# The last two head pairs of slot attention inside the opening order of cross-attention

## The chip, the cores and the metric

The kernel runs on one core of a Trainium2 chip. The metric is the device time of one execution in microseconds (us). TensorE (PE) multiplies; PEld is its weight load, which runs beside it. VectorE (DVE), ScalarE (ACT) and GpSimd (POOL) work on what it leaves in the eight PSUM banks, and SyncE (SP) issues DMAs. Every engine runs its own instruction stream in order, and the streams meet only at semaphores.

## The reference, cut to what matters

One decoder layer on x of 8 sequences x 128 tokens x 256 channels:

```
x = x + slot_attention(layernorm(x))     # 16 heads of 128, 64 slots
x = x + cross_attention(layernorm(x), ctx)   # 32 heads of 8
x = x + experts(layernorm(x))            # 8 experts (2 chosen) + 1 shared
```

Slot attention, for each head (q and k have rotary positions):

```
s  = clip(hs @ Ws1.T @ Ws2.T + bs2);  es = exp(s);  enz = 1 / cumsum(es)
ok = enz * (mask(q k^T) @ es)
W2 = mask((softmax(ok) * enz) @ es^T)
o  = rmsnorm(W2 @ v) * silu(g);  y += o @ Wo.T
```

## The kernel before

The 16 heads are worked on as 8 pairs, the 8 sequences of a pair in 4 groups of two. A pair has projection steps and attention steps. Projections fill a PSUM bank each: QK 0 to 7 (q and k, each then rotated by VectorE and GpSimd), VG 0 to 7 (v and gate of a sequence), ST and SN (slot scores, both ways), CS 0 and 1 (running sums of es). ScalarE takes a logarithm of CS, then an exponential, to get `enz`; before it, it loads the table set that has the logarithm, and after CS 1 the set that has the tanh of VG. The attention steps of group g are, on TensorE: A (q k^T), E (times es), T (transpose), W (W2), O (times v), OT (transpose), Y (times Wo, in three products of high and low parts). Between them other engines mask, scale, exponentiate, square and norm. All A write bank 2, E and Y share bank 3, T and OT share bank 4, W uses bank 5, and O banks 6 and 7 in turn. Tiles between the engines have two buffers, chosen by the group's number modulo 2.

Every engine has a list of steps written out in its order. In turn i of the loop (`Fori(1, PAIRS - 2)`) the attention of pair i runs beside the projections of pair i + 1. After the loop one more turn of the same order is written out for pair 6 (with the projections of pair 7). Then come lists of the next stage: `X_PE_START`, `X_DVE_START`, `X_ACT_START`, `X_POOL_START` and `X_SP_START`, here called the opening. They hold the attention of pair 7 (steps "7A" to "7Y", "7N2" the second norm's statistics) mixed with the first steps of cross-attention for sequences 0, 1 and 2. These are G 0 to 6 (projections and the stacks of q and k, turned), H (norm), L1 (logits, whose maxima VectorE takes: line 1458), TT (the maxima turned), a DMA that puts them into the rows of q (`QT`, line 1278), L2 (logits again, less the maxima; ScalarE exponentiates them), AV, AB, AT and OUT (the output), S3, HN and HT (third norm), and GT, the first expert product (from line 1395 on). WH and WL split the experts' weights of expert b into high (ScalarE) and low parts (GpSimd, lines 1680 and 1681). After GT of sequence 0 the regular turns `X_PE` begin, one for each sequence.

The steps of the opening that need a free PSUM bank are `FILLERS`; `bank_plan()` hands out the bank that has been free longest, so banks 0 and 1 first and the others when the attention has left them (`FREED`). Raw weights of the next stage lie in places of tiles that the projections leave. The steps FREE and LATE of SyncE wait until the last projection is through (`projections_done`) and then issue nine DMAs in a row, 4.1 MB. Line 248 to 250 are the three products of high and low parts wherever they occur.

## Time and profile before

| | |
|---|---|
| runs of the kernel (3) | 610.56, 611.94, 614.62 us; median 611.94 |
| profiled execution, its own time | 614.3 us |
| its span, first to last instruction | 612.5 us |
| busy share of the span | PE 95%, DVE 79%, ACT 60%, POOL 46% |
| mean granted TensorE clock | 0.983 |

All times within an execution count from the start of its span. A clock of 1.00 is 2.4 GHz, and 0.5 is 1.2 GHz. The busy time of TensorE includes the drain of a matmul, which overlaps the next one, so a busy share of 0.9 is less work than 0.9 of the stretch, and at half clock the same work shows as twice the busy time.

### The profile page before, as it was taken

How to read it: one execution, taken by the hardware profiler on the slowest of the kernel's cores; microseconds unless marked ns; L12 is line 12 of the kernel's file. 1: busy time of each engine (PE TensorE's matmuls, PEld its weight loads, DVE VectorE, ACT ScalarE, POOL GpSimd, SP SyncE). 2: the span in 40 equal slices, each digit the busy share in tenths (PEclk: the TensorE clock that was granted, in tenths of full speed). 3: DMA queues.
4: the chain of work that ended last, by engine and by line, in shares of the span. 5: the costliest groups of instructions: out<-in, count | busy, mean ns of one | idle time of the engine just before them, and what ended most of it. 6: DMA issues, size and time to landing. Idle time of an engine off the chain costs nothing.

```text
span 612.5 us, 14139 instructions
## 1 busy us (share of the span) xinstructions
PE 581.9 (95%) x4426; PEld 490.9 (80%) x4426; DVE 486.6 (79%) x1150; ACT 369.8 (60%) x1166; POOL 281.9 (46%) x324
## 2 busy tenths in 40 slices
PE   5989999999999999999999999986889999999998
PEld 5868888888888888888888888774668878877786
DVE  5999978887977977977986986775687887886776
ACT  3448566647657557557567555756666576567453
POOL 3366844754845755663663664545562211220000
PEclk9999999999999999999999999987799999999999
DMA  8200101101100100200200000700000000000000
GB/s 273 70 0 34 55 1 39 50 1 34 51 0 32 54 0 0 86 0 0 86 0 1 18 2 1 276 2 1 3 3 11 2 12 11 3 11 12 3 10 18
DMA packets 10321, 19.35 MB, mean 32 GB/s; under 512 B 2336, under 2 KB 5920, under 8 KB 10144
## 3 DMA queue, kind: packets, MB, share of 16 engines
q1 hardware_dynamic: 10272, 18.74, 8.9%
q8 instruction: 26, 0.43, 0.3%
q14 instruction: 23, 0.19, 0.1%
HBM read 17.55 MB, written 1.05 MB: 30 GB/s over the span
## 4 chain that ended last, share of the span: by engine, by line
PE 81%; DVE 8%; issue 5%; DMA 2%; POOL 1%; ACT 1%; SPq 1%; DVEq 0%; POOLq 0%; ACTq 0%
PE bank L248 16%; PE bank L250 15%; PE bank L249 15%; PE bank L589 4%; PE bank L546 3%; PE bank L1359 3%; PE bank L581 3%; PE bank L558 3%; PE bank L599 2%; PE bank L1288 2%; PE bank L1348 2%; PE bank L1336 2%; PE bank L1407 1%; PE bank L1306 1%; PE bank L1366 1%
## 5 line engine op out<-in xcount | busy, mean ns | idle before, releaser
L845 ACT ACTIVATE sa_v<-bank 128x256 f32<-128x256 f32 x64 | 24.4, 382 | 66.9 <-PE bank L250 66.8
L908 POOL TENSOR_TENSOR sa_qt<-sa_rope_cos,sa_rope_sin 128x512 f32<-128x512 f32 x32 | 41.2, 1286 | 42.2 <-DVE sa_rope_sin L760 42.0
L819 ACT ACTIVATE sa_ex<-sa_okb,sa_minus_top 128x64 f32<-128x64 f32 x128 | 42.9, 339 | 24.9 <-DVE sa_minus_top L712 24.9
L248 PE MATMUL bank<-ht_hi,sa_qk_hi 128*128 128x512 f32 x128 | 55.4, 432 | 1.0 <-DVE sa_gate L765 0.9
L908 POOL TENSOR_TENSOR sa_kt<-sa_rope_cos,sa_rope_sin 128x512 f32<-128x512 f32 x32 | 41.2, 1289 | 30.7 <-DVE sa_rope_sin L760 30.7
L248 PE MATMUL bank<-sa_vg_hi,ht_hi 128*128 128x512 f32 x128 | 52.6, 411 | 0.5 <-DVE sa_rope_sin L760 0.5
L250 PE MATMUL bank<-sa_vg_hi,ht_lo 128*128 128x512 f32 x128 | 50.5, 395 | 0.0
L250 PE MATMUL bank<-ht_hi,sa_qk_lo 128*128 128x512 f32 x128 | 50.5, 394 | 0.0
L249 PE MATMUL bank<-sa_vg_lo,ht_hi 128*128 128x512 f32 x128 | 50.5, 394 | 0.0
L249 PE MATMUL bank<-ht_lo,sa_qk_hi 128*128 128x512 f32 x128 | 50.2, 392 | 0.0
L758 DVE TENSOR_TENSOR sa_rope_cos<-bank,con 128x512 f32<-128x512 f32 x64 | 44.0, 687 | 6.0 <-PE bank L250 5.5
L1458 DVE TENSOR_REDUCE xf_neg_top<-bank 128x4 f32<-128x512 f32 x64 | 40.3, 682 | 9.3 <-PE bank L1336 9.1
L759 DVE TENSOR_TENSOR sa_rope_sin<-bank,con 64x512 f32<-64x512 f32 x64 | 44.3, 692 | 0.9
L760 DVE TENSOR_TENSOR sa_rope_sin<-bank,con 64x512 f32<-64x512 f32 x64 | 43.8, 684 | 0.8
L1657 POOL TENSOR_TENSOR xf_rot<-xf_by_cos,xf_by_sin 128x256 f32<-128x256 f32 x16 | 12.1, 756 | 65.2 <-DVE xf_by_sin L1451 65.2
L914 POOL TENSOR_TENSOR sa_qe<-sa_ex,sa_enz 128x256 f32<-128x256 f32 x32 | 23.4, 731 | 39.2 <-ACT sa_ex L819 39.2
L1557 ACT ACTIVATE xf_wt<-bank 128x512 f32<-128x512 f32 x64 | 34.1, 600 | 8.1 <-PE bank L1348 8.1
L248 PE MATMUL bank<-sa_wo_hi,sa_ogt_hi 128*128 128x256 f32 x128 | 38.4, 300 | 0.0
L831 ACT ACTIVATE sa_junk<-bank 128x128 f32<-128x128 f32 x128 | 33.7, 282 | 6.5 <-PE bank L589 6.5
L765 DVE SCALAR_TENSOR_TENSOR sa_gate<-sa_th,bank 128x256 f32<-128x256 f32 x64 | 26.5, 417 | 13.6 <-ACT sa_th L848 5.7
L546 PEld LDWEIGHTS bank<-sa_qt,sa_kt 128*128 128x128 f32 x256 | 32.3, 191 | 5.8 <-DVE sa_att L703 3.7
L726 DVE SCALAR_TENSOR_TENSOR sa_og<-bank,sa_rms,sa_gate 128x128 f32<-128x128 f32 x128 | 35.8, 343 | 1.3 <-POOL sa_rms L927 1.1
(207 smaller groups left out, 1840.7 us busy)
## 6 DMA issues: line engine op xcount, KB each, us to landing
sa_qk_raw<-in_wqk SPq DMA_DIRECT2D x8, 512.0 KB, 3.8
sa_vg_raw<-in_wvg SPq DMA_DIRECT2D x8, 512.0 KB, 3.2
sa_wo_raw<-in_wo SPq DMA_DIRECT2D x8, 256.0 KB, 2.7
xf_w_raw<-in_w SPq DMA_DIRECT2D x2, 640.0 KB, 11.1
xf_w_raw<-in_w SPq DMA_DIRECT2D x1, 1152.0 KB, 9.6
xs<-in_x SPq DMA_DIRECT2D x2, 512.0 KB, 4.6
hn<-in_w SPq DMA_DIRECT2D x2, 512.0 KB, 4.9
out<-xs SPq DMA_DIRECT2D x8, 128.0 KB, 1.7
```

What stands on the lines that cost most here:

```text
L248: pe.matmul(out, w_hi, m_hi, start=first, stop=False)
L249: pe.matmul(out, w_hi, m_lo, start=False, stop=False)
L250: return pe.matmul(out, w_lo, m_hi, start=False, stop=last)
L546: mm = pe.matmul(ps_a[:, u * TOK:(u + 1) * TOK], kt[:, h, b * TOK:(b + 1) * TOK], qt[:, h, b * TOK:(b + 1) * TOK], start=True, stop=True)
L726: ins = dve.scalar_tensor_tensor(out=og[:, s, u, :], in0=ps_o[s][:, u * DK:(u + 1) * DK], scalar=rms[:, s, u:u + 1], in1=gate[:, b, h * DK ...
L758: dve.tensor_tensor(rope_cos[:, s, :].rearrange("p (b t) -> p b t", b=4), psv, cos4, ALU.mult)
L759: dve.tensor_tensor(rs[0:64], psv[64:128], sin4[64:128], ALU.mult)
L760: dve.tensor_tensor(rs[64:128], psv[0:64], sin4[0:64], ALU.mult).then_inc(draining, 1)
L819: ins = act.activation(ex[:, s, u, :], okb[:, s, u, :], ACT.Exp, bias=minus_top[:, s, u:u + 1], accum_out=total[:, g, u:u + 1])
L908: pool.tensor_tensor(dst[:, h, c * HALF:(c + 1) * HALF], rope_cos[:, s, :], rope_sin[:, s, :], ALU.add).then_inc(roped, 1)
L1458: dve.tensor_reduce(neg_top[:, b % 2, n % 4, 4 * (n // 4):4 * (n // 4) + 4], bank(filled(step, n, b), 0, 512, 4), AX.X, ALU.max, negate=Tr ...
L1557: act.activation(wt[:, n, :, :], bank(filled(step, n, b), 0, 512, 4), ACT.Exp, scale=XDIM ** -0.5).then_inc(exp_done, 1)
```

## The change

The turn of pair 6 is no longer a turn of the loop's order. Its steps, attention of pair 6 and projections of pair 7, stand in the opening's lists as "6A", "6QK" and so on, and all lists of the opening are new orders. Attention goes by groups across both pairs in the order `LAST_ORDER`: 6.0, 6.1, 6.2, 7.0, 7.1, 6.3, 7.2, 7.3. The counters of the semaphores and the choice of the buffer of two follow that order (`group`, `at`, `buffer_of`). As E and Y, and T and OT, of the two pairs now mix, each waits for whatever stood before it in its shared bank (`shared_banks`). Pair 7 has its own buffer of `wo_hi` and `wo_lo` (`wo_set`). The projections of pair 7 become fillers with banks from `bank_plan()`. CS 0 and CS 1 stand apart on ScalarE with VG steps between them, so that each gets its own load of the logarithm's table set and is followed by one of the tanh's set.

The tiles `qk_hi`, `qk_lo`, `rope_cos` and `rope_sin` moved into the region that is freed late. So the DMAs of the next stage fall into two lots: FREE (wq, the first four experts' w1 and w3, gate) after CS 1, and LATE (bout, w2, wout, the other experts' w1 and w3: 2.8 MB) once VG 7 and QK 7 are through.

Core of the diff:

```diff
@@ -79,49 +79,50 @@
 LEAD = 4
 
 
-def at(i, g):
-
-    return 4 * i + g + 1 + LEAD
-
-
-LATE = {"VG": 8, "QK": 8}
-
-
-def is_late(f):
-
-    return f[1] >= LATE.get(f[0], 8)
-
-
-PLACE_LAST = {f: n for n, f in enumerate([f for f in FILLS if not is_late(f)])}
+LAST_ORDER = ((6, 0), (6, 1), (6, 2), (7, 0), (7, 1), (6, 3), (7, 2), (7, 3))
+
+
+def group(i, g):
+
+    if isinstance(i, int) and i >= PAIRS - 2:
+        return 4 * (PAIRS - 2) + LAST_ORDER.index((i, g))
+    return 4 * i + g
+
+
+def at(i, g, back=0):
+
+    return group(i, g) + 1 + LEAD - back
+
+
+def buffer_of(i, g, k):
+
+    return group(i, g) % k if isinstance(i, int) else g % k
+
+
+LATE = {"VG": 0, "QK": 0}
...
+def wo_set(i):
+
+    return 1 if isinstance(i, int) and i == PAIRS - 1 else 0
+
+
+def apart_sums():
+
+    names = [(step, n) for step, n, b in X_ACT_START]
+    return any(step in ("6VG", "U", "GT") for step, n in names[names.index(("6CS", 0)):names.index(("6CS", 1))])
+
+
+def shared_banks():
+
+    before, last = {}, {"E": ("Y", 3, PAIRS - 3), "T": ("OT", 3, PAIRS - 3)}
+    for step, n, b in X_PE_START:
+        if step in LAST_TWO and LAST_TWO[step][0] in ("E", "Y", "T", "OT"):
+            which, i = LAST_TWO[step]
+            kind = "E" if which in ("E", "Y") else "T"
+            before[which, n, i], last[kind] = last[kind], (which, n, i)
+    return before
...
     with engine.Fori(1, PAIRS - 2) as i:
-        run(i, attend=True, project=True, split_qk=True)
-    run(PAIRS - 2, attend=True, project=True, split_qk=False)
-
-
-    def last_pair(step, n, ps=None):
-
-        if step in PROJECTING:
-            run(PAIRS - 2, attend=True, project=True, split_qk=False, only=[(step, n)], given=ps)
-        else:
-            run(PAIRS - 1, attend=True, project=False, split_qk=False, only=[(step, n)])
-
-    return last_pair
+        run(i, attend=True)
+
+
+    def last_two(step, n, i, ps=None):
+
+        run(i, attend=True, only=[(step, n)], given=ps)
+
+    return last_two
...
     qk_raw, vg_raw = sb("qk_raw", [P, KC, 512]), sb("vg_raw", [P, KC, 512])
-    qk_hi, qk_lo = sb("qk_hi", [P, KC, 512], F32R), sb("qk_lo", [P, KC, 512], F32R)
-    rope_cos, rope_sin = sb("rope_cos", [P, 2, HALF]), sb("rope_sin", [P, 2, HALF])
...
     vg_hi, vg_lo = sb("vg_hi", [P, KC, 512], F32R), sb("vg_lo", [P, KC, 512], F32R)
+    qk_hi, qk_lo = sb("qk_hi", [P, KC, 512], F32R), sb("qk_lo", [P, KC, 512], F32R)
+    rope_cos, rope_sin = sb("rope_cos", [P, 2, HALF]), sb("rope_sin", [P, 2, HALF])
     th = sb("th", [P, 2, 2 * DK])
...
-    wo_hi, wo_lo = sb("wo_hi", [P, 2, DIM], F32R), sb("wo_lo", [P, 2, DIM], F32R)
+    wo_hi, wo_lo = sb("wo_hi", [P, 2, 2, DIM], F32R), sb("wo_lo", [P, 2, 2, DIM], F32R)
...
+        def wait_shared(before):
+            step, g, i = before
+            drained_by = {"E": scaled, "Y": added, "T": qet_done, "OT": ogt_lo_done}
+            pe.wait_ge(drained_by[step], at(i, g))
...
                     pe.wait_ge(es_done, 2 * i + g // 2 + 1)
-                    pe.wait_ge(scaled, at(i, g - 1))
-                    if g == 0:
-                        pe.wait_ge(added, at(i, -1))
+                    if before is not None:
+                        wait_shared(before)
+                    else:
+                        pe.wait_ge(scaled, at(i, g, 1))
...
                     pe.wait_ge(qe_done, at(i, g))
-                    if g == 0:
-                        pe.wait_ge(ogt_lo_done, at(i, -1))
+                    if before is not None:
+                        wait_shared(before)
+                    elif g == 0:
+                        pe.wait_ge(ogt_lo_done, at(i, 0, 1))
                     else:
-                        pe.wait_ge(qet_done, at(i, g - 1))
...
                     pe.wait_ge(ogt_lo_done, at(i, g))
-                    pe.wait_ge(added, at(i, g - 1))
                     if g == 0:
-                        pe.wait_ge(scaled, at(i, 3))
                         pe.wait_ge(wo_lo_done, i + 2)
+                    if before is not None:
+                        wait_shared(before)
+                    else:
+                        pe.wait_ge(added, at(i, g, 1))
+                        if g == 0:
+                            pe.wait_ge(scaled, at(i, 3))
+                    k = wo_set(i)
                     for b in range(2):
                         for h in range(2):
                             u = 2 * b + h
-                            mm = split_product(pe, ps_y[:, b * DIM:(b + 1) * DIM], ogt_hi[:, g % 2, u, :], ogt_lo[:, g % 2, u, :],
-                                               wo_hi[:, h, :], wo_lo[:, h, :], h == 0, h == 1)
+                            mm = split_product(pe, ps_y[:, b * DIM:(b + 1) * DIM], ogt_hi[:, s, u, :], ogt_lo[:, s, u, :],
+                                               wo_hi[:, k, h, :], wo_lo[:, k, h, :], h == 0, h == 1)
                     mm.then_inc(y_ready, 1)
...
+                if (step, n) == ("CS", 0) or (step, n) == ("CS", 1) and isinstance(r, int) and r == PAIRS - 1 and apart_sums():
                     act.preload_act_table_set("natural_log_exp_and_others")
...
                     act.wait_ge(wo_scaled, i + 2)
-                    act.wait_ge(y_ready, at(i, -1))
-                    act.activation(wo_hi[:, :, :], wo[:, :, :], ACT.Copy).then_inc(wo_hi_done, 1)
+                    if not wo_set(i):
+                        act.wait_ge(y_ready, at(i, 0, 1))
+                    act.activation(wo_hi[:, wo_set(i), :, :], wo[:, :, :], ACT.Copy).then_inc(wo_hi_done, 1)
...
-        engine.wait_ge(fill, filled(PAIRS - 1, ("CS", 1)))
-        engine.wait_ge(drain, NDRAIN * (PAIRS - 1) + len(PLACE_LAST) - 2)
+        for f in [(step, 1) for step in ("ST", "SN", "CS")] + [(step, n - 1) for step, n in LATE.items() if n]:
+            wait_filled(engine, PAIRS - 1, f)
+            wait_drained(engine, PAIRS - 1, f)
         engine.wait_ge(enz_done, 2 * PAIRS)
+        engine.wait_ge(es_t_done, 2 * PAIRS)
+        engine.wait_ge(qk_lo_done, PAIRS)
+        engine.wait_ge(vg_lo_done, PAIRS)
         engine.wait_ge(roped, 8 * (PAIRS - 1) + LATE["QK"])
 
     def late_done(engine):
 
         for step in LATE:
-            if LATE[step] < 8:
-                wait_filled(engine, PAIRS - 1, (step, 7))
-                wait_drained(engine, PAIRS - 1, (step, 7))
+            wait_filled(engine, PAIRS - 1, (step, 7))
+            wait_drained(engine, PAIRS - 1, (step, 7))
         engine.wait_ge(roped, 8 * PAIRS)
...
+X_PE_START = [("6QK", 0, 6), ("6A", 0, 6), ("6QK", 1, 6), ("6E", 0, 6), ("6A", 1, 6), ("6ST", 0, 6), ("6QK", 2, 6),
+    ("6E", 1, 6), ("6A", 2, 6), ("6T", 0, 6), ("6SN", 0, 6), ("6W", 0, 6), ("6ST", 1, 6), ("6QK", 3, 6),
+    ("6QK", 4, 6), ("6O", 0, 6), ("6T", 1, 6), ("6E", 2, 6), ("6W", 1, 6), ("6CS", 0, 6), ("7A", 0, 7), ("6QK", 5, 6),
+    ("7A", 1, 7), ("7E", 0, 7), ("6O", 1, 6), ("6OT", 0, 6), ("7E", 1, 7), ("6VG", 0, 6), ("6A", 3, 6), ("6SN", 1, 6),
+    ("6Y", 0, 6), ("6VG", 1, 6), ("6T", 2, 6), ("6E", 3, 6), ("7T", 0, 7), ("6W", 2, 6), ("6QK", 6, 6), ("6OT", 1, 6),
+    ("7W", 0, 7), ("6O", 2, 6), ("6QK", 7, 6), ("6VG", 2, 6), ("7O", 0, 7), ("7T", 1, 7), ("6Y", 1, 6), ("6CS", 1, 6),
+    ("6OT", 2, 6), ("6VG", 3, 6), ("7W", 1, 7), ("7A", 2, 7), ("6T", 3, 6), ("6Y", 2, 6), ("6W", 3, 6), ("7OT", 0, 7),
+    ("6VG", 4, 6), ("7E", 2, 7), ("7A", 3, 7), ("7O", 1, 7), ("7Y", 0, 7), ("G", 0, 0), ("7E", 3, 7), ("6O", 3, 6),
+    ("6VG", 5, 6), ("7T", 2, 7), ("G", 1, 0), ("6VG", 6, 6), ("7T", 3, 7), ("7W", 2, 7), ("G", 2, 0), ("7OT", 1, 7),
+    ("7O", 2, 7), ("6VG", 7, 6), ("7W", 3, 7), ("6OT", 3, 6), ("G", 3, 0), ("7Y", 1, 7), ("G", 4, 0), ("G", 5, 0),
+    ("G", 6, 0), ("7O", 3, 7), ("L1", 0, 0), ("7OT", 2, 7), ("G", 0, 1), ("G", 1, 1), ("6Y", 3, 6), ("L1", 1, 0),
+    ("G", 2, 1), ("7OT", 3, 7), ("7Y", 2, 7), ("G", 3, 1), ("TT", 0, 0), ("G", 4, 1), ("G", 5, 1), ("7Y", 3, 7),
+    ("G", 6, 1), ("G", 0, 2), ("G", 1, 2), ("L2", 0, 0), ("G", 2, 2), ("L2", 1, 0), ("AV", 0, 0), ("L1", 0, 1),
+    ("AB", 0, 0), ("AV", 1, 0), ("L1", 1, 1), ("AB", 1, 0), ("AT", 0, 0), ("G", 3, 2), ("OUT", 0, 0), ("TT", 0, 1),
+    ("G", 4, 2), ("HT", 0, 0), ("G", 5, 2), ("G", 6, 2), ("GT", 0, 0)]
...
+X_DVE_START = [("6QK", 0, 6), ("6A", 0, 6), ("6QK", 1, 6), ("6E", 0, 6), ("6A", 1, 6), ("6ST", 0, 6), ("6QK", 2, 6),
+    ("6SN", 0, 6), ("6E", 1, 6), ("6ST", 1, 6), ("6A", 2, 6), ("6W", 0, 6), ("6QK", 3, 6), ("6QK", 4, 6),
+    ("6E", 2, 6), ("7A", 0, 7), ("6W", 1, 6), ("6O", 0, 6), ("7A", 1, 7), ("7E", 0, 7), ("6QK", 5, 6), ("6OT", 0, 6),
+    ("7E", 1, 7), ("6SN", 1, 6), ("6VG", 0, 6), ("6Y", 0, 6), ("6A", 3, 6), ("6O", 1, 6), ("6W", 2, 6), ("6VG", 1, 6),
+    ("6QK", 6, 6), ("6E", 3, 6), ("7W", 0, 7), ("6OT", 1, 6), ("6QK", 7, 6), ("6O", 2, 6), ("6VG", 2, 6),
+    ("6Y", 1, 6), ("6OT", 2, 6), ("7O", 0, 7), ("6VG", 3, 6), ("7W", 1, 7), ("6Y", 2, 6), ("6W", 3, 6), ("7A", 2, 7),
+    ("7E", 2, 7), ("7OT", 0, 7), ("FREE", 0, 0), ("7A", 3, 7), ("7Y", 0, 7), ("6VG", 4, 6), ("7N2", 0, 7),
+    ("7E", 3, 7), ("G", 0, 0), ("H", 0, 0), ("7O", 1, 7), ("6VG", 5, 6), ("7W", 2, 7), ("G", 2, 0), ("6O", 3, 6),
+    ("7OT", 1, 7), ("H", 0, 1), ("6VG", 6, 6), ("6VG", 7, 6), ("7W", 3, 7), ("7O", 2, 7), ("7Y", 1, 7), ("7N2", 1, 7),
+    ("6OT", 3, 6), ("L1", 0, 0), ("L1", 1, 0), ("L1", 2, 0), ("L1", 3, 0), ("G", 0, 1), ("7O", 3, 7), ("L1", 4, 0),
+    ("6Y", 3, 6), ("7OT", 2, 7), ("G", 2, 1), ("L1", 5, 0), ("L1", 6, 0), ("L1", 7, 0), ("7Y", 2, 7), ("7OT", 3, 7),
+    ("7N2", 2, 7), ("7Y", 3, 7), ("H", 0, 2), ("G", 0, 2), ("G", 2, 2), ("L1", 0, 1), ("L1", 1, 1), ("L1", 2, 1),
+    ("L1", 3, 1), ("DV", 0, 0), ("L1", 4, 1), ("DV", 1, 0), ("L1", 5, 1), ("L1", 6, 1), ("L1", 7, 1), ("OUT", 0, 0),
...
+X_POOL_START = [("6VGLO", 0, 6), ("6WO", 0, 6), ("6QK", 0, 6), ("6E", 0, 6), ("6QK", 1, 6), ("6QK", 2, 6),
+    ("6SUM", 0, 6), ("6E", 1, 6), ("6SN", 0, 6), ("6QK", 3, 6), ("6WOLO", 0, 6), ("6SUM", 1, 6), ("6MS", 0, 6),
+    ("6E", 2, 6), ("7WO", 0, 7), ("7E", 0, 7), ("6SUM", 2, 6), ("6QK", 4, 6), ("7SUM", 0, 7), ("6MS", 1, 6),
+    ("7SUM", 1, 7), ("6QK", 5, 6), ("7E", 1, 7), ("6QK", 6, 6), ("6SN", 1, 6), ("6MS", 2, 6), ("6QK", 7, 6),
+    ("7MS", 0, 7), ("6E", 3, 6), ("7WOLO", 0, 7), ("6SUM", 3, 6), ("FREE", 0, 0), ("7N2", 0, 7), ("7E", 2, 7),
+    ("7MS", 1, 7), ("7E", 3, 7), ("7SUM", 2, 7), ("ROT", 0, 0), ("6MS", 3, 6), ("7SUM", 3, 7), ("LO", 0, 0),
+    ("ROT", 1, 0), ("7MS", 2, 7), ("LO", 1, 0), ("7MS", 3, 7), ("ROT", 0, 1), ("LO", 0, 1), ("7N2", 1, 7),
+    ("ROT", 1, 1), ("BIAS", 0, 0), ("LO", 1, 1), ("7N2", 2, 7), ("WL", 0, 0), ("BIAS", 0, 1), ("ROT", 0, 2),
+    ("BIAS", 0, 2), ("WL", 1, 1), ("ROT", 1, 2), ("LO", 0, 2), ("WL", 2, 2), ("WL", 3, 3), ("S3", 0, 0), ("LO", 1, 2),
+    ("WL", 4, 4), ("7N2", 3, 7), ("WL", 5, 5), ("WL", 6, 6), ("WL", 7, 7), ("WL", 8, 8)]
...
+                    sp.dma_start(gate_raw[:, :, :], a["gate"]).then_inc(gate_in, 16)
+                elif step == "LATE":
+
+                    slots.late_done(sp)
+                    sp.dma_start(bout[:, :], a["bout"].to_broadcast([P, DIM])).then_inc(bout_in, 16)
+                    sp.dma_start(w2_raw[:, :, :], a["w2"]).then_inc(w2_in, 16)
                     sp.dma_start(wout[:, :, :], a["wout"]).then_inc(wout_in, 16)
-                    sp.dma_start(bout[:, :], a["bout"].to_broadcast([P, DIM])).then_inc(bout_in, 16)
-                    sp.dma_start(gate_raw[:, :, :], a["gate"]).then_inc(gate_in, 16)
-                    sp.dma_start(w2_raw[:, :, :], a["w2"]).then_inc(w2_in, 16)
-                elif step == "LATE":
-
-                    slots.late_done(sp)
                     for kc in range(KC):
                         sp.dma_start(w13_raw[:, kc, :, :], a["w13"][:, kc, RAW:NE, :]).then_inc(w13_in2, 16)
...
                     act.wait_ge(pe_at, done(b))
+                    if b == 0:
+                        slots.late_done(act)
```

On ScalarE the opening now has the order ... 6VG 4, 7O 1, ..., 6VG 7, HI 1 of sequence 0, 6OT 3, G 3 to 6, 7O 3, ..., G 6 of sequence 1, WH 0, G 1 and V of sequence 2, WH 1, L2 0 to 6, ..., WH 2, WH 3, and the other WH to the end. The loop's turns 1 to 5, the regular turns and the last turn are the same as before.

## Rows read from the trace of the kernel before

**Rows 1.** Page, parts 1 and 2: whole execution; clock in 40 slices.

```profile
PE 581.9 (95%) x4426; PEld 490.9 (80%) x4426; DVE 486.6 (79%) x1150; ACT 369.8 (60%) x1166; POOL 281.9 (46%) x324
...
PEclk9999999999999999999999999987799999999999
```

**Rows 2.** Stretches: engines' busy time (instructions), granted clock, DMA share, GB/s.

```profile
332.00:444.70 112.70, 99.62 (x760) 82.97 (x760) 81.12 (x189) 71.12 (x242) 60.41 (x81) 0.92 0.12 41
332.00:379.70 47.70, 47.38 (x311) 40.82 (x311) 39.57 (x81) 28.43 (x104) 26.53 (x30) 1.00 0.02 7
379.70:413.20 33.50, 29.24 (x219) 25.17 (x217) 23.21 (x66) 22.13 (x89) 15.97 (x28) 0.95 0.35 127
404.00:409.00 5.00, 4.79 (x24) 4.67 (x25) 2.94 (x10) 1.92 (x5) 3.37 (x5) 0.66 0.00 0
418.50:425.10 6.60, 1.19 (x9) 0.95 (x9) 2.95 (x8) 6.21 (x15) 5.78 (x8) 0.79 0.01 3
425.10:437.00 11.90, 11.86 (x141) 8.35 (x142) 4.70 (x11) 8.23 (x18) 6.26 (x8) 0.55 0.00 1
437.00:444.70 7.70, 4.80 (x30) 3.42 (x29) 5.54 (x15) 4.08 (x11) 3.67 (x5) 1.00 0.02 4
```

**Rows 3.** Chain of waits: start, duration, engine, line, instructions (steps at full clock).

```profile
331.99 0.89 PE bank L546 x8
...
340.67 0.84 PE bank L558 x8
...
361.49 0.65 PE bank L581 x8
...
366.05 0.44 PE bank L599 x4
...
444.72 0.36 PE bank L248
...
455.69 0.87 PE bank L1316 x4
...
457.00 1.01 PE bank L1359 x32
458.01 0.65 PE bank L1336 x16
```

**Rows 4.** Timeline of TensorE at the opening: start, duration, instruction [idle before <-releaser].

```profile
377.80 0.28 PE L248 MATMUL bank<-sa_wo_hi,sa_ogt_hi 128*128 128x256 f32 x1
...
379.23 0.40 PE L649 MATMUL bank<-sa_es_hi,sa_tri_r 128*128 128x512 f32 x1
...
413.16 0.67 PE L1336 MATMUL bank<-xf_kt,xf_qt 32*128 32x128 f32 x16
...
420.40 0.27 PE L1327 MATMUL bank<-con,xf_neg_top 128*32 128x128 f32 x1 [2.01 <-DVE xf_neg_top L1458]
...
425.14 1.12 PE L1348 MATMUL bank<-xf_qt,xf_kt 32*128 32x128 f32 x16 [3.55 <-DMA xf_qt<-xf_neg_top_t]
```

**Rows 5.** Timeline of VectorE: maxima of the cross-attention's logits.

```profile
417.77 2.49 DVE L1458 TENSOR_REDUCE xf_neg_top<-bank 128x4 f32<-128x512 f32 x4
```

**Rows 6.** Timeline of ScalarE at the last table load before the opening.

```profile
377.82 0.38 ACT L848 ACTIVATE sa_th<-bank 128x256 f32<-128x256 f32 x1
378.21 1.28 ACT L797 ACT_TABLE_LOAD   x1
379.51 0.60 ACT L870 ACTIVATE sa_log_cs<-bank 128x512 f32<-128x512 f32 x1
```

**Rows 7.** Timeline of GpSimd: experts' weights, and one norm step.

```profile
420.18 1.28 POOL L1680 TENSOR_TENSOR xf_w_lo<-hn,xf_w_hi 128x512 fp32r<-128x512 f32 x1
421.41 0.74 POOL L1681 TENSOR_TENSOR xf_w_lo<-xf_w_raw,xf_w_hi 128x256 fp32r<-128x256 f32 x1
...
441.72 0.56 POOL L1668 TENSOR_TENSOR xf_rstd<-xf_var_eps,xf_minus_half 128x1 f32<-128x1 f32 x1 [1.32 <-DVE xf_var_eps L1485]
```

**Rows 8.** DMA issues from SyncE: destination, count, size, median us to landing.

```profile
xf_w_raw<-in_w SPq DMA_DIRECT2D x2, 640.0 KB, 11.1
```

188 lines of the change are left out of this document (94 added, 94 removed), and 43 rows, old and new, of tables (X_ACT_START, X_DVE_START, X_PE_START, X_POOL_START).

## Prediction

> **What bounds the kernel now.** I began with the page: TensorE is busy for 95% of the span at a granted clock of 0.9 or more in nearly all slices, with one dip in slices 27 to 29, between 400 and 445 us [rows 1]. So the kernel is bound by TensorE's stream nearly everywhere, and the question is what happens at that dip. The stretches show it. In the turn of pair 6, 332.0 to 379.7 us, TensorE is busy 47.38 of 47.70 us at full clock, VectorE 39.57. In the opening behind it nothing is full: 379.7 to 413.2 at 29.24 of 33.50 us, then 1.19 of 6.60 us around 420, then 11.86 of 11.90 but at clock 0.55, then 4.80 of 7.70 [rows 2]. The timeline names the waits of the last part: TT waits 2.01 us for VectorE's maxima, L2 waits 3.55 us for the little DMA that puts the maxima into q [rows 4].
>
> How much work is in the opening? I price steps at full clock from the chain of waits, where pieces do not overlap: A and O 0.89 us (the same eight matmuls), E 0.84, W 0.65, OT 0.44, G 2 and OUT 0.87, AV 1.01, L1 and L2 0.65 [rows 3]; Y takes 379.23 - 377.80 = 1.43 [rows 4]. Pair 7 is four times (0.89 + 0.84 + 0.65 + 0.89 + 0.44 + 1.43, and 0.28 for T by half an OT and a little) = 21.7 us. Cross-attention up to GT is 14 steps of four transposes at 0.44 (12 G, 2 AB), four at 0.87 (3 G 2, OUT), six L1 and L2 at 0.65, two AV at 0.97, three G 0 at about 0.46 (two matmuls of 512 columns) and 1.3 for the seven small ones: 18.3 us. Together 40 us of work, and the opening lasts from 379.7 to 444.7, 65.0 us. So 25 us are lost there, to waits and to the half clock. That is all the change can win. With pair 6 the stage has 47.7 + 40 = 87.7 us of work in 112.7.
>
> Where it is lost: until the first L1 at 413.16 [rows 4] the work is 24.2 us of 33.5 (73%), since pair 7's attention is a chain of short steps with little beside it. From L1 to GT it is 15.8 us of work in 31.6.
>
> **The change, part by part.** It removes no arithmetic and adds none. The loop of pairs 1 to 5, the regular turns and the end are as before. I put nothing down for them.
>
> The merged part. The projections of pair 7, dense work until now only beside pair 6, are now spread over 6VG and 6QK steps that reach down to the last group of pair 7, and the first cross-attention steps come among them. I walked the new order of TensorE with the prices above. From 6QK 0 to the start of 7Y 3 there are 74.7 us of work; from 7Y 3 to GT there are 13.0. The first 16 us, up to the first 7A, are the loop's mixture. The turn of pair 6 shows what such a mixture costs: 0.3 us of idle in 47.7 [rows 2]. The opening shows the other bound, 9.3 us lost in 24.2 of work. The new mixture is nearer to the turn, because a projection or a G stands between most dependent steps. For the 58.7 us after the first 7A, bounds are 0.4 us (the turn's share) and 22 us (the opening's 73%). I take 1.5 us, apart from the wait at TT below.
>
> VectorE is the engine to fear there. In the whole stage it is busy 81.1 us [rows 2] against 87.7 us of TensorE's work, so a stage shortened to 98 leaves it 83% busy, as in the pair's turn now (39.57 of 47.70). But at the first L1 it gets much at once: eight maxima at 2.49/4 = 0.62 us [rows 5], two G at 0.8, and five attention drains and scalings, together 9 to 10 us, while TensorE has 7.0 us of work between L1 and TT (L1 twice, 7OT 2, 7OT 3, 6Y 3, 7Y 2, G 0 to G 3 of sequence 1). So TT waits about 2.5 us, as long as it does now (2.01) [rows 4]. Queued behind TT on TensorE are G 4, G 5 and 7Y 3, and behind 7Y 3 the release of WH and WL.
>
> TT to L2 is 4.74 us now (425.14 - 420.40) [rows 4], with 0.9 us of work in it. Now 3.5 us stand there (G 4, G 5, G 6, 7Y 3, G 0 and G 1 of sequence 2). The round trip stays, so 1.2 us are left idle instead of 3.55.
>
> The tail, from 7Y 3 to GT, has two chains. One is L2, exponentials, AV, AB, AT, OUT, S3: 441.72 - 425.14 = 16.6 us now [rows 4, 7], 11.9 of it at clock 0.55 where 11.86 x 0.55 = 6.5 us of work ran [rows 2]. At full clock 5.3 us fewer: 11.3. L2 starts 4.2 us after 7Y 3 (TT to L2 less the 0.9 us between TT and 7Y 3, with some slack), so S3 is at 15.5. The other is GpSimd: WH 0 waits for 7Y 3 to be added (2.3 us), takes 1.0, and then four WL at 1.28 + 0.74 = 2.02 [rows 7] and five steps of 0.7 (BIAS, ROT, LO) stand before S3: 2.3 + 1.0 + 8.1 + 3.6 = 15.0. They are even. From S3 to GT is 444.72 - 441.72 = 3.0 us [rows 3, 7]. The tail is 18.5 us; now it is 30.6 from 7Y 3 (414.1) on.
>
> Edits with a small answer. 6QK 0 now stands ahead of 6A 0, and its bank 0 is free only when the logarithm of CS 0 is through: a table load of 1.28 us and 0.60 us [rows 6] against Y 3 and CS 1, 1.7 us, which leaves 0.3 to 0.9 us of wait. I take 0.6. The second set of `wo_hi` and `wo_lo` takes away the wait of 7WOHI for pair 6's Y; on TensorE nothing waited for it, so nothing, and without it pair 7's Y could not stand before 6Y 3. The wait of WO for `wo_lo_done` is for an instruction long past on the same engine: nothing. Unlinked CS 0 and CS 1: two more table loads on ScalarE, 2 x 1.28 = 2.6 us; ScalarE is busy 71.1 of 112.7 us [rows 2], so it is hidden, except where exponentials of E stand behind it. At most 2.6, at least nothing; I take nothing, as each has 1 to 2 us of TensorE's work ahead of its readers. In this trace the load begins when the activation before it ends and the next activation follows at once (378.20, 378.21, 379.49, 379.51) [rows 6]. The Trainium skill, ScalarE: Activation LUTs, section What ACT_TABLE_LOAD costs, charges a drain of about 1.38 us on top of each switch. The trace does not show it here; by the page the two loads would be 5.3 us of ScalarE and the forecast perhaps a microsecond later.
>
> The clock. It was down in 404 to 409 (0.66) and again after 418.5 to 425.1, where TensorE was busy 1.19 us of 6.60, and then 11.9 us ran at half clock [rows 2]. The new order has no stretch as empty as that, but its tail holds 11.6 us of work in 17 to 18. The bounds are nothing and 5.3 us. I take 1.1.
>
> The sum: 74.7 + 0.6 + 1.5 + 2.5 + 18.5 + 1.1 = 98.9 us for the stage that takes 112.7. The gain is 13.8 us. The profiled execution took 614.3 us, its span 612.5 with 1.8 around it, so it would take 600.5. It lies 2.4 us above the median of the runs; from the median, 611.94, it is 598.1. I say 599.
>
> **The rivals.** First, the clock falls again in the tail. For it: the tail still has a dependent chain with work for two thirds of it, and in 404 to 409 the clock was down although TensorE had been busy for most of the time since 379.7. Against it: over 379.7 to 413.2, at 73% of work, the clock's mean was still 0.95 [rows 2]. The price is 5.3 us less the 1.1 in the sum, so 603.
>
> Second, the ring of the little DMA. The LATE lot, 2.8 MB, is now issued when 6VG 7 is drained, and between that and TT lie 11.8 us of TensorE's work plus the waits. The two 640 KB transfers landed 11.1 us after issue, behind a like amount [rows 8]. So if TT comes early, QT's four DMAs meet it. The Trainium skill, DMA: Bandwidth & Descriptors, section Queues, rings and completion order, says that descriptors of one issuing engine are taken in ring order on each DMA engine, which speaks against the change here; no row of this trace shows a small transfer behind a large one. Worked out from the rows: lot issued about 2 us after VG 7 and landed 12 us later, TT's copy 15 us after VG 7, so L2 is late by 0 to 2 us, which gives 601.
>
> Third, slower. TensorE takes its list in order, and in the merged part E and Y of two pairs take turns in bank 3, T and OT in bank 4, 32 uses in all, each behind the drain of the one before; both pairs' groups must also pass every engine in one order, with two buffers. If the orders do not fit the real times, each such step stops everything behind it. It decides by the density of the 58.7 us after the first 7A: 16 + 58.7/x + 18.5 equals 112.7 at x = 75%. Pair 7's attention now runs at 73% with the same steps. At 68% it would be 120.8 us, 8 more than now: 620. Half of it, x = 80%, is 107.9, a gain of 4.8: 607. Against it: in the pair's turn the same steps with the same banks run at 99% [rows 2], and the new order has projections down to its last fifth.
>
> Fourth, better than I say: TT finds its maxima ready and the tail's two chains overlap with the weights earlier, which gives 2.5 + 2 us more, 594.
>
> **How the numbers follow.** Forecast, 594.5 to 602: 0.50. Clock, 602 to 605: 0.18. The little DMA, about 601: 0.06. Better, below 594.5: 0.10. Half density, 606 to 612: 0.11. Slower, above 618: 0.05. Faster by over 1% (below 605.8), which is about what a measurement of this kernel can tell from no change, is the sum of the first four, 0.84; within 1% 0.11; slower 0.05. The range leaves out the slow case, half of the half density and part of the better one: 593 to 607.
>
> **What the profile after would show.** Right: the end of pair 5's turn still at 332 us and GT about 431; TensorE busy over 95% at clock 1.00 from 332 to about 405; no stretch of several us with TensorE under a third busy; the waits of TT and L2 together about 4 us instead of 5.6; S3 of GpSimd right behind the fourth WL. Wrong: waits of E, Y, T, OT for VectorE or ScalarE of over 5 us in sum in the merged part; a clock of 0.5 behind L2; L2 waiting for the DMA for over 4 us; and, if the stage does end near 431, a first regular turn that gives the gain back, because TensorE waits there for `w_lo_done` of the late experts.

## The result and the profile after

The changed kernel takes 604.98 us (median of 4 runs, 604.03 to 605.19), the kernel before 611.70 in the same comparison (4 runs, 610.56 to 614.62). The ratio is 0.988, with an interval from 0.9851 to 0.9908: faster by 1.2%, 6.7 us. Forecast were 599 us and a gain of 12.7 to 13.8. The profiled execution after took 605.02 us, its span is 603.2; against the profiled one before (614.3 and 612.5) it is 9.3 us shorter.

From the page of the kernel after, the lines that answer to [rows 1]:

```profile
span 603.2 us, 14152 instructions
...
PE 578.4 (96%) x4426; PEld 487.8 (81%) x4426; DVE 485.5 (80%) x1150; ACT 371.6 (62%) x1168; POOL 282.4 (47%) x324
...
PEclk9999999999999999999999999999989999999999
```

The dip in the clock that filled three slices is now one.

The view of stretches of the kernel after: start and end, length, busy us and count of TensorE (matmul, then weight load), VectorE, ScalarE and GpSimd, granted clock, DMA share, GB/s. It answers to [rows 2].

```profile
331.86:379.70 47.84, 46.19 (x320) 39.62 (x320) 40.34 (x82) 31.42 (x115) 28.13 (x33) 1.00 0.03 7
379.70:399.00 19.30, 18.63 (x131) 15.51 (x132) 13.24 (x40) 15.43 (x61) 10.10 (x20) 1.00 0.22 70
399.00:414.70 15.70, 14.39 (x133) 12.16 (x129) 14.57 (x38) 8.80 (x28) 7.19 (x10) 1.00 0.51 185
414.70:418.50 3.80, 3.32 (x22) 2.38 (x21) 2.02 (x7) 2.40 (x7) 0.94 (x3) 1.00 0.02 4
418.50:434.60 16.10, 10.85 (x165) 8.28 (x165) 9.85 (x24) 14.28 (x35) 14.08 (x17) 0.99 0.01 3
434.60:440.90 6.30, 6.26 (x29) 4.42 (x30) 4.04 (x20) 4.99 (x13) 0.95 (x2) 0.50 0.00 1
```

From 331.86 to 414.70 TensorE is busy 79.21 of 82.84 us at full clock; no stretch is left like the 1.19 of 6.60 around 420. The tail from 418.5 to 434.6 holds 10.85 us in 16.1. Then comes what was not in the sum: the first 6.3 us of the first regular turn run at clock 0.50, with TensorE busy all the time.

TensorE's timeline of the kernel after, at the waits and steps that answer to [rows 4]: start, duration, line, what, and in brackets the idle time before it with its releaser.

```profile
332.32 0.50 PE L266 MATMUL bank<-ht_hi,sa_qk_hi 128*128 128x512 f32 x1 [0.29 <-ACT sa_log_cs L909]
...
336.89 1.10 PE L587 MATMUL bank<-sa_es,sa_att 128*128 128x64 f32 x8 [0.63 <-DVE sa_att L741]
...
356.64 1.08 PE L587 MATMUL bank<-sa_es,sa_att 128*128 128x64 f32 x8 [0.62 <-DVE sa_okb L747]
...
386.25 0.35 PE L266 MATMUL bank<-sa_wo_hi,sa_ogt_hi 128*128 128x256 f32 x1 [0.66 <-issue]
...
387.76 1.02 PE L1369 MATMUL bank<-wkv,ctx_all 128*128 128x512 f32 x2
388.79 1.08 PE L587 MATMUL bank<-sa_es,sa_att 128*128 128x64 f32 x8
...
404.12 0.67 PE L1399 MATMUL bank<-xf_kt,xf_qt 32*128 32x128 f32 x16
...
409.68 1.13 PE L1379 MATMUL bank<-xf_wq,xf_h2t 128*128 128x256 f32 x4 [0.76 <-DVE xf_neg_top L1521]
...
413.61 0.27 PE L1390 MATMUL bank<-con,xf_neg_top 128*32 128x128 f32 x1
...
414.72 0.39 PE L266 MATMUL bank<-sa_wo_hi,sa_ogt_hi 128*128 128x256 f32 x1
...
418.52 0.67 PE L1411 MATMUL bank<-xf_qt,xf_kt 32*128 32x128 f32 x16 [0.50 <-DMA xf_qt<-xf_neg_top_t]
...
433.25 0.41 PE L1446 MATMUL bank<-con,hn 128*128 128x128 f32 x2 [2.41 <-DVE hn L1553]
...
434.64 0.56 PE L266 MATMUL bank<-xf_w_hi,ht_hi 128*128 128x264 f32 x1
```

L1 stands at 404.12 (before 413.16), TT at 413.61 (420.40), 7Y 3 at 414.72, L2 at 418.52 (425.14), GT at 434.64 (444.72). GT comes 10.1 us earlier. Counted from 331.86, where the stage begins here, it takes 102.8 us, before 112.7, and 3.9 more than the 98.9 forecast. From GT to the end of the span it is 168.6 us, before 167.8.

### The profile page after: what moved, and what is told of

Read it like the earlier page. It is cut to its first block and busy times, and to the rows that moved or that the text cites. A ratio compares the mean times of both kernels' runs of the same rounds, so it can differ in the third digit from the quotient of the medians.

```text
span 603.2 us, 14152 instructions
## 1 busy us (share of the span) xinstructions
PE 578.4 (96%) x4426; PEld 487.8 (81%) x4426; DVE 485.5 (80%) x1150; ACT 371.6 (62%) x1168; POOL 282.4 (47%) x324
## 5 line engine op out<-in xcount | busy, mean ns | idle before, releaser
L267 PE MATMUL bank<-sa_wo_lo,sa_ogt_hi 128*128 128x256 f32 x128 | 36.1, 282 | 0.0
```

Source lines behind the costliest of these rows:

```text
L267: pe.matmul(out, w_hi, m_lo, start=False, stop=False)
```

## The experiments

Three questions: is the gain the order's, or another edit's or the clock's; what makes up the 3.9 us that are missing; and was the ring of the little DMA ever near. In the table, starts in us are those of the profiled execution; "rest" is the time from GT to the end of the span, and "clock" is the mean granted clock of the whole execution. The stage itself begins up to 0.5 us earlier or later from one execution to the next (the last matmul ahead of it stands at 331.63 in after, 331.34 in a_first, 331.41 in cs0_early and tail2, 331.11 in loads_more), so differences of a few tenths between marks are read from there. Each ratio is taken against runs of the kernel before on the same chip in the same session.

| kernel | median us | ratio (interval) | L1 | TT | L2 | GT | rest | clock |
|---|---|---|---|---|---|---|---|---|
| before | 611.70 | 1 | 413.16 | 420.40 | 425.14 | 444.72 | 167.8 | 0.983 |
| after | 604.98 | 0.988 (0.985 to 0.991) | 404.12 | 413.61 | 418.52 | 434.64 | 168.6 | 0.992 |
| old_order | 612.76 | 1.000 (0.998 to 1.002) | 413.31 | 420.53 | 425.27 | 444.43 | 166.4 | 0.986 |
| before_keep | 613.03 | 1.002 (1.001 to 1.004) | 411.97 | 420.39 | 426.75 | 443.88 | 166.6 | 1.000 |
| after_keep | 604.35 | 0.987 (0.985 to 0.990) | 403.98 | 413.48 | 418.38 | 434.44 | 166.5 | 1.000 |
| cross_last | 630.23 | 1.031 (1.027 to 1.036) | 425.40 | 433.76 | 438.60 | 454.87 | 171.3 | 0.978 |
| a_first | 604.71 | 0.987 (0.984 to 0.990) | 403.92 | 413.41 | 418.32 | 437.21 | 167.1 | 0.992 |
| loads_more | 612.74 | 1.001 (0.999 to 1.004) | 410.74 | 420.23 | 425.14 | 444.08 | 167.1 | 0.986 |
| cs0_early | 604.02 | 0.987 (0.985 to 0.989) | 403.03 | 412.52 | 417.44 | 436.31 | 167.1 | 0.992 |
| tail2 | 606.14 | 0.990 (0.988 to 0.992) | 403.88 | 413.06 | 419.94 | 437.96 | 166.4 | 0.993 |
| all_edits | 604.29 | 0.987 (0.985 to 0.989) | 402.82 | 412.01 | 418.88 | 435.22 | 166.5 | 0.999 |
| lot_more | 603.85 | 0.987 (0.983 to 0.991) | 403.78 | 413.27 | 418.21 | 434.37 | 168.6 | 0.992 |
| lot_most | 619.74 | 1.012 (1.009 to 1.016) | 403.87 | 413.36 | 433.07 | 452.27 | 167.0 | 0.978 |

**The kernel before, once more.** The kernel of [rows 1] to [rows 8], unchanged.

> The kernel before, unchanged, for a second profile of it. If the profiled execution shown with the case was an ordinary one, the opening again ends (GT of sequence 0) near 444.7 us with half-clock stretches of about 16 us in all. If it was a slow example, the half-clock stretches are shorter and GT comes 2 us earlier, which would explain why the profiled executions differ by 9.3 us and the medians only by 6.7.

This execution took 612.92 us with a span of 611.1; GT at 444.35 against 444.72. The stretches of half clock stand at the same places: 0.95 over 379.7 to 413.2, 0.66 over 404 to 409, 0.63 over 418.5 to 437. So up to GT the profiled execution before was an ordinary one. The difference lies near the end: over 563 to 572 the granted clock was 0.81 in the execution of the rows and 1.00 in this one, and the first is 1.4 us longer (614.3 against 612.92), all of it behind 551. 23 runs of the kernel before on one chip lay between 610.30 and 616.29, median 611.73; the 614.3 of the profiled one belongs to the upper part. That is why the profiled pair differs by 9.3 us and the medians by 6.7.

**The order alone.** All of the changed kernel but its order: groups and lists as before.

```diff
-LAST_ORDER = ((6, 0), (6, 1), (6, 2), (7, 0), (7, 1), (6, 3), (7, 2), (7, 3))
+LAST_ORDER = ((6, 0), (6, 1), (6, 2), (6, 3), (7, 0), (7, 1), (7, 2), (7, 3))
-X_PE_START = [("6QK", 0, 6), ("6A", 0, 6), ("6QK", 1, 6), ("6E", 0, 6), ("6A", 1, 6), ("6ST", 0, 6), ("6QK", 2, 6),
+X_PE_START = [("6A", 0, 6), ("6QK", 0, 6), ("6A", 1, 6), ("6E", 0, 6), ("6SN", 0, 6), ("6ST", 0, 6), ("6A", 2, 6),
...
```

> The changed kernel's code with the old order: pair 6 whole in the loop's order, then the old lists of the opening; LAST_ORDER sequential. Theory: the whole gain is the order, so this is the time of the kernel before, within 1 us (611 to 612). Rival: the split of the DMAs into two lots, the second set of output weights and the changed waits are worth something by themselves; then it lies 1.5 us or more from the kernel before, and the order's share differs by that.

612.76 us, ratio 0.9999 (0.9976 to 1.0022), and every mark within 0.3 us of the kernel before. The second set of output weights, the tiles that moved, the two lots of DMAs and the new counters cost nothing and bring nothing that this run can tell from noise. The gain is the order's. (The two added table loads are not in this kernel, as CS 0 and CS 1 stand together in the old order.)

**Cross-attention behind attention.** The order of after, with the steps of cross-attention's first sequence taken out of the merged part and set behind 7Y 3 on all engines.

```diff
-    ("6VG", 4, 6), ("7E", 2, 7), ("7A", 3, 7), ("7O", 1, 7), ("7Y", 0, 7), ("G", 0, 0), ("7E", 3, 7), ("6O", 3, 6),
...
+    ("6OT", 3, 6), ("7Y", 1, 7), ("7O", 3, 7), ("7OT", 2, 7), ("6Y", 3, 6), ("7OT", 3, 7), ("7Y", 2, 7), ("7Y", 3, 7),
+    ("G", 0, 0), ("G", 1, 0), ("G", 2, 0), ("G", 3, 0), ("G", 4, 0), ("G", 5, 0), ("G", 6, 0), ("L1", 0, 0),
...
```

> The changed kernel with each engine's opening list split: all steps of pairs 6 and 7 first, in the changed order, then all cross-attention steps, in their order. Theory: mixing the pairs makes the attention dense by itself (69 us of TensorE's work in about 76), and the other half of the gain is that cross-attention's chain of 35 us lies beside it; so this loses most of the gain and ends at 610 to 614. Rival: the pairs' mixture alone is the gain, and the cross-attention steps only move along; then 603 to 607. In its profile the last Y of pair 7 stands near 408 us by the theory.

630.23 us, ratio 1.0313: 25 us slower than after and 18.5 slower than before. The last Y begins at 412.60, only 2.1 us before that of after, while GT is at 454.87, 42.3 us behind it. Stretches of this kernel, columns as above:

```profile
380.00:400.00 20.00, 18.18 (x134) 15.43 (x133) 12.32 (x36) 14.76 (x59) 8.80 (x17) 1.00 0.20 68
400.00:405.00 5.00, 3.09 (x27) 2.93 (x27) 4.12 (x15) 1.77 (x10) 1.87 (x3) 1.00 0.86 203
405.00:415.00 10.00, 7.15 (x36) 5.91 (x35) 4.72 (x12) 0.60 (x1) 0.69 (x1) 0.66 0.46 188
415.00:430.00 15.00, 9.37 (x60) 6.20 (x60) 6.89 (x22) 4.92 (x12) 3.95 (x6) 0.77 0.00 0
```

Where nothing is left to fill with, TensorE is busy 3.09 of 5.00 us and then 9.37 of 15.00, and the clock is down at 0.66 and 0.77. Merged attention with nothing of cross-attention among it loses 18.5 us against the kernel before; it wins only with cross-attention's long chain beside it. The kernel before had a mixture of its own, which this run takes away too. So what merging the pairs is worth while that old mixture stays, no run shows.

**The clock held up in the kernel before.** Transposes that nobody reads were put where TensorE idled (after the wait for the bank, so in a bank that is rewritten).

```diff
+KEEP = {('G', 1, 0): 9, ('G', 2, 0): 4, ('TT', 0, 0): 16, ('L2', 0, 0): 30, ('AT', 0, 0): 6, ('OUT', 0, 0): 4, ('HT', 0, 0): 14}
...
+                    for _ in range(KEEP.get((step, n, b), 0)):
+                        pe.transpose(ps[:, 0:TOK], ident, ident)
```

> The kernel before with idle transposes added on TensorE, into the bank that the next step will fill anyway, ahead of G 1, G 2, TT, L2, AT, OUT and HT of sequence 0 (83 in all, each about 0.11 us at full clock), where TensorE would wait. Theory (the change gained by filling waits, and by the clock as well): holding the clock alone gives 4 to 6 us of the 5.3 + 2 us that half clock costs, so 606 to 608. Rival (the clock is hidden behind the chain of latencies): no gain, 611 to 613. Second rival (the clock is nearly the whole gain of the change): 605 or less.

The granted clock was 1.00 for the whole profiled execution, and the kernel took 613.03 us (12 runs, 611.98 to 614.14), ratio 1.002: nothing won. L2 to GT fell from 19.6 us to 17.1, so the half clock there had cost about 2.5 us, not the 5.3 of the prediction, and L1 came 1.2 us earlier, which is the fall over 404 to 409. But TT and L2 lost this, as TensorE's timeline of this kernel shows:

```profile
418.59 1.97 PE L1301 MATMUL bank<-con 128*128 128x128 f32 x16 [1.39 <-ACT xf_kt L1579]
420.39 0.27 PE L1330 MATMUL bank<-con,xf_neg_top 128*32 128x128 f32 x1
...
423.35 3.46 PE L1301 MATMUL bank<-con 128*128 128x128 f32 x30 [1.81 <-ACT xf_kt L1579]
426.75 0.67 PE L1351 MATMUL bank<-xf_qt,xf_kt 32*128 32x128 f32 x16
```

VectorE's last maxima were through at 419.04, but the 16 transposes ahead of TT got their bank only at 418.59 and held TT up to 420.39, where it stood before. The 30 ahead of L2 waited for their bank until 423.35 and held L2 up to 426.75, 1.6 us later than before. So idle matmuls give the clock's price back unless they end in time, and this run does not bound the clock's share by nothing: 1.2 us up to L1 and 2.5 behind L2 are an estimate of what the full clock is worth in the kernel before, 3.7 us. The changed order has the full clock at both places, so up to 3.7 of the 10.1 us by which GT comes earlier can be the clock's. The rest is the waits'. In a_first below the clock falls in the tail, and GT still stands 7.5 us ahead of the kernel before.

**The clock held up in the changed kernel.** The same with 6 transposes ahead of AT, 18 ahead of HT and 2 ahead of OUT.

```diff
+KEEP = {('AT', 0, 0): 6, ('HT', 0, 0): 18, ('OUT', 0, 0): 2}
```

> The changed kernel with 26 idle transposes ahead of AT, OUT and HT of sequence 0. Theory: the fall of the clock at GT (434.6 us, half clock for 6.3 us) costs 3 us and comes from the waits at AT and HT, so this gains 2 to 3 us: 602 to 603. Rival: the regular turn behind it has slack that takes the half clock up, or the transposes delay the chain; then 604.5 to 606.

604.35 us; the interval of its ratio, 0.985 to 0.9895, overlaps that of after. In the profiled execution the clock was 1.00 throughout, GT at 434.44, and the rest 166.5 us instead of 168.6. These 2.1 us are two falls, as the steps TT in the regular turns show, first of after, then of after_keep:

```profile
452.99 0.27 PE L1390 MATMUL bank<-con,xf_neg_top 128*32 128x128 f32 x1
...
542.03 0.27 PE L1390 MATMUL bank<-con,xf_neg_top 128*32 128x128 f32 x1
```

```profile
451.83 0.27 PE L1393 MATMUL bank<-con,xf_neg_top 128*32 128x128 f32 x1
...
540.89 0.27 PE L1393 MATMUL bank<-con,xf_neg_top 128*32 128x128 f32 x1
```

The next TT stands at 564.30 in after and at 561.95 in after_keep. So after is 0.20 us behind at GT, 1.16 at 452.99, 1.14 at 542.03 and 2.35 at 564.30. The half clock behind GT costs 1.0 us, and a second fall near the end (0.79 over 555 to 563, where after_keep has 1.00) costs 1.2. The single runs, by their mean clock, us:

| kernel | 0.999 or 1.000 | 0.997 | 0.991 to 0.994 |
|---|---|---|---|
| after | none | 604.03 | 604.94, 605.02, 605.19 |
| after_keep | 602.78, 602.93 | 604.33, 604.38 | 604.71, 604.83 |
| a_first | 602.66 | 604.01, 604.89 | 604.57, 604.84, 606.11 |
| lot_more | 602.90, 602.92 | none | 604.77, 605.25 |
| cs0_early | none | 603.12 | 604.00, 604.03, 605.23 |
| tail2 | none | 605.99, 606.04 | 606.24, 607.00 |
| all_edits | 603.52, 603.88, 604.70 | none | 605.55 |
| before_keep | 611.98 to 612.33 (6) | 613.74, 613.97 | 613.84 to 614.14 (4) |

In most of these kernels the runs without a fall lie some 1 to 2 us below the others; in all_edits the gap is not clean. That the transposes hold the clock is not shown in the changed kernel: with them 2 of 6 runs had no fall, without them 1 of 6 in a_first and 2 of 4 in lot_more. In the kernel before they do raise it: all 12 runs with them are at 0.994 or more, the 23 without at 0.983 to 0.992.

**6A 0 ahead of 6QK 0.** The first item of TensorE's and VectorE's lists changed places with the second, so that the wait for the logarithm of CS 0 is filled.

```diff
-X_PE_START = [("6QK", 0, 6), ("6A", 0, 6), ("6QK", 1, 6),
+X_PE_START = [("6A", 0, 6), ("6QK", 0, 6), ("6QK", 1, 6),
```

> The changed kernel with 6A 0 ahead of 6QK 0 on TensorE and VectorE, as in the loop. The trace after has waits of 0.45 us at 6QK 0 and 0.8 us at 6E 0. Theory: both come from that order, so GT comes about 1 us earlier (433.6) and the time is 604. Rival: behind it VectorE and the drains set the pace and the first microsecond is made up by other waits before 7Y 3; then GT stays within 0.3 us of 434.6.

604.71 us, L1 0.20 us earlier, L2 0.20 us, and the stage itself began 0.3 us earlier, so nothing was won. A wait of 0.92 us for VectorE's rope took the place of those at 6QK 0 and 6E 0:

```profile
338.33 0.50 PE L266 MATMUL bank<-ht_hi,sa_qk_hi 128*128 128x512 f32 x1 [0.92 <-DVE sa_rope_sin L798]
```

In the first 19.3 us VectorE is busy 16.81 (16.72 in after). Up to L2 the rival was right: VectorE's work sets the pace at the beginning of the merged part. In this execution the clock fell inside the tail (0.76 over 418.3 to 437.2). L2 to GT took 18.9 us, 2.8 more than the 16.1 of after_keep, and the rest 167.1, 0.6 more. Together that is 3.4 us, as much as lies between this execution, 606.11, and the one at full clock, 602.66.

**Two more table loads at each CS.** Ahead of the load of the logarithm's set at CS 0 and at CS 1 of pair 7's turn, two further loads.

```diff
+                    if isinstance(r, int) and r == PAIRS - 1:
+                        act.preload_act_table_set("natural_log_exp_and_others")
+                        act.preload_act_table_set("exp_and_others")
                     act.preload_act_table_set("natural_log_exp_and_others")
```

> The changed kernel with two more table loads ahead of each of CS 0 and CS 1 of pair 7 on ScalarE (four loads, 5.1 us more of ScalarE). Theory (the forecast's nothing for the two loads that the change adds): 1 us or less, 604.5 to 606. Rival: ScalarE's loads hold up E and T of the mixed part, and then each costs TensorE most of its 1.28 us: 608 to 610, and the change's own two loads are 2 to 2.5 us of the 4 by which the mixed part was slower than forecast.

612.74 us, 7.8 over after: the four loads, 5.1 us of ScalarE, ate the whole gain. ScalarE's timeline of this kernel, at CS 0:

```profile
352.88 1.28 ACT L836 ACT_TABLE_LOAD   x1
354.17 1.28 ACT L837 ACT_TABLE_LOAD   x1
355.45 1.28 ACT L838 ACT_TABLE_LOAD   x1
356.75 0.60 ACT L912 ACTIVATE sa_log_cs<-bank 128x512 f32<-128x512 f32 x1
```

and TensorE's, where it waited for it:

```profile
358.66 1.08 PE L587 MATMUL bank<-sa_es,sa_att 128*128 128x64 f32 x8 [3.19 <-DVE sa_okb L747]
...
387.24 0.79 PE L266 MATMUL bank<-sa_vg_hi,ht_hi 128*128 128x512 f32 x1 [2.31 <-ACT sa_log_cs L912]
```

The wait of 7E 1 grew from 0.62 to 3.19 us, which is the two loads, 2.6; at CS 1 a wait of 2.31 appeared where there was none. L1 came 6.6 us later, so more was lost than these 4.9: TensorE's clock was 0.93 over 355 to 380 and 0.91 over 379.7 to 399.0, which the kernel after has at 1.00. With the added loads ScalarE is at both places on the path, though it is busy for 62% of the span only. A load takes 1.28 us, loads stand back to back, and the next activation begins 0.02 us behind. The Trainium skill, ScalarE: Activation LUTs, section What ACT_TABLE_LOAD costs, adds a drain of about 1.38 us to each switch; the trace does not agree.

**CS 0 ahead of 6E 2.** On ScalarE alone, CS 0 with its load is done before the exponentials of 6E 2, not behind them.

```diff
-    ("6O", 0, 6), ("6WOHI", 0, 6), ("6E", 2, 6), ("6CS", 0, 6), ("6OT", 0, 6), ("7E", 0, 7), ("6ST", 0, 6),
+    ("6O", 0, 6), ("6WOHI", 0, 6), ("6CS", 0, 6), ("6E", 2, 6), ("6OT", 0, 6), ("7E", 0, 7), ("6ST", 0, 6),
```

> The changed kernel with 6CS 0 ahead of 6E 2 on ScalarE. In the trace after, ScalarE idles 1.52 us ahead of 6E 2 and then loads the logarithm's table (1.28 us) for CS 0, and 7E 1 of TensorE waits at 356.6 us for what follows. Theory: the load is on the path there, so putting it into the idle time takes away the wait of 0.8 us: everything from L1 on comes 0.5 to 0.8 us earlier. Rival: 6E 2 comes later by as much and 6A 3 or 6T 2 wait instead: no gain or a loss of up to 1 us.

ScalarE's timeline of this kernel around the moved step:

```profile
349.56 0.66 ACT L880 ACTIVATE sa_wo_hi<-sa_wo 128x512 fp32r<-128x512 f32 x1
350.23 1.28 ACT L835 ACT_TABLE_LOAD   x1
351.52 0.60 ACT L909 ACTIVATE sa_log_cs<-bank 128x512 f32<-128x512 f32 x1
...
355.81 0.60 ACT L875 ACTIVATE sa_ogt_hi<-bank 128x512 fp32r<-128x512 f32 x1 [1.70 <-PE bank L632]
```

The same load now lies in time that ScalarE would have waited: behind it and the exponentials, 1.70 us are left idle before `ogt_hi`, where in after the load stood between the exponentials (352.99) and `ogt_hi` (356.06) with no gap. The wait of 7E 1 is gone, and L1, TT and L2 are 1.1 us earlier, 0.9 of it since the stage's start. So CS 0 with its load at that place had cost 0.9 us. It is not one of the two loads that the change adds: a load ahead of CS 0 stood in the kernel before too, at 378.21, behind the projections. The median is 604.02; a difference of 1.0 us is not clear of the noise, and in the profiled execution the clock fell in the tail, with GT at 436.31.

**Four moves in the tail.** WH 1 behind the exponentials of L2 on ScalarE, AB 1 ahead of the next sequence's L1 on TensorE, DV 1 and the last three maxima earlier on VectorE.

```diff
-    ("AB", 0, 0), ("AV", 1, 0), ("L1", 1, 1), ("AB", 1, 0), ("AT", 0, 0), ("G", 3, 2),
+    ("AB", 0, 0), ("AV", 1, 0), ("AB", 1, 0), ("L1", 1, 1), ("AT", 0, 0), ("G", 3, 2),
-    ("6Y", 3, 6), ("7OT", 2, 7), ("G", 2, 1), ("L1", 5, 0), ("L1", 6, 0), ("L1", 7, 0), ("7Y", 2, 7),
+    ("6Y", 3, 6), ("7OT", 2, 7), ("L1", 5, 0), ("L1", 6, 0), ("L1", 7, 0), ("G", 2, 1), ("7Y", 2, 7),
-    ("L1", 4, 1), ("DV", 1, 0), ("L1", 5, 1),
+    ("DV", 1, 0), ("L1", 4, 1), ("L1", 5, 1),
-    ("V", 0, 2), ("WH", 1, 1), ("L2", 0, 0), ... ("L2", 6, 0), ("AC", 0, 0),
+    ("V", 0, 2), ("L2", 0, 0), ... ("L2", 6, 0), ("WH", 1, 1), ("AC", 0, 0),
```

> The changed kernel with four steps moved: WH 1 behind the L2 exponentials on ScalarE, AB 1 ahead of L1 1 of sequence 1 on TensorE with its division (DV 1) ahead of a maximum on VectorE, and G 2 of sequence 1 behind the last maxima of sequence 0 on VectorE. Theory (the tail is a chain through ScalarE's exponentials and VectorE's maxima, 1.4 us longer than forecast): TT 0.8 us earlier, L2 0.5, GT 1.5 to 2.5 us earlier, 602.5 to 604. Rival (GpSimd's weight splits stand right behind it): GT at most 0.7 us earlier, because WL 2 and WL 3 come later with WH 1, S3 waits for them.

606.14 us, 1.2 over after, with intervals that overlap. TT was 0.55 us earlier (0.3 since the stage's start), as meant, but 7Y 3 1.3 us later (415.99). The groups of this kernel's instructions between 408 and 416 us (busy time, mean ns, idle time before them and its releasers) show why:

```profile
L1351 PE MATMUL bank<-con,xf_stack 128*128 128x128 f32 x12 | 1.8, 274 | 1.8 <-POOL xf_stack L1726 1.8
```

G 2 of sequence 1, moved behind three maxima, made its stack late on GpSimd; G 4 and G 5 wait for that stack, and 7Y 3 and L2 are queued behind them on TensorE. My theory looked at who waits for the maxima and not at who waits for the step that they passed.

**All edits that had seemed to help.** CS 0 early, the four moves and the transposes of after_keep together.

> The last two kernels' moves together with the 26 idle transposes ahead of AT, OUT and HT. Theory: the parts add, 0.7 + 2 + 0.6 to 2 us: 600.5 to 602.5. Rival: the shorter tail leaves GpSimd's WL as the bound and they don't add: 603 to 604.

604.29 us, with TT at 412.01 but L2 at 418.88 and GT at 435.22: what CS 0 gives, the moves of the tail take. No version is clearly better than after: the medians of a_first, cs0_early, after_keep, all_edits and lot_more lie between 603.85 and 604.71, beside 604.98, and their intervals overlap with that of after.

**A larger lot ahead of the little DMA.** A copy of the experts' weights into a tile in memory that nobody reads, 2.4 MB on SyncE's queue between the LATE lot and QT.

```diff
+                    for kc in range(KC):
+                        sp.dma_start(spare[:, kc, :, :], a["w13"][:, kc, 0:NE, :]).then_inc(spare_in, 16)
```

> The changed kernel with 2.36 MB more behind the LATE lot on SyncE's queue, copied to a spare tensor in DRAM (extra work, not used). In the trace after, the lot has landed at about 410.4 us and the four little DMAs of QT start at 414.4, so they met nothing. By the second rival's mechanism they now wait for the extra copy, which ends at about 420 to 425: L2 of sequence 0 moves from 418.5 to 422 or later and the kernel to 608 or more. If a small transfer passes the large ones, L2 stays at 418.5 to 419.5 and the time within 1 us of 605.

603.85 us and L2 at 418.21 with a wait of 0.53: no delay. The copy had ended at about 416 (its DMAs landed 12.9 us after their issue, 402.2 to 403.7), while QT's DMAs were issued from 414.05 to 416.4, so they hardly met. It tells nothing about the order of the queue, only that there was room for 2.4 MB more.

**Three times that lot.**

```diff
+                    for copy, kc in [(c, k) for c in range(3) for k in range(KC)]:
+                        sp.dma_start(spare[copy, :, kc, :, :], a["w13"][:, kc, 0:NE, :]).then_inc(spare_in, 16)
```

> As the kernel with 2.36 MB more behind the LATE lot, but three times as much, 7.1 MB, so that the queue is busy until about 425 to 430 us. (In the run with 2.36 MB the extra copy was over at 417, only 1 to 3 us after QT's first DMA was issued, and L2 did not move.) If the little DMAs wait their turn behind it, L2 of sequence 0 goes from 418.5 to 427 or later and the kernel to 612 or more. If they pass, L2 stays at 418 to 419.5.

619.74 us. The chain of waits of this kernel between 414 and 434 us (start, us, what):

```profile
415.69 0.64 SPq L1344
416.32 0.04 issue
416.37 16.56 DMA xf_qt<-xf_neg_top_t
432.93 0.14 issue
433.07 1.08 PE bank L1415 x12
```

The last of the four DMAs of 4 KB took 16.56 us; in the chain of the kernel before, with nothing ahead of it, it takes 1.78. It landed when the copy was through (the DMA engines' busy share is 0.26 over 430 to 432 and 0.00 over 432 to 434). So a little transfer does wait behind the large ones issued before it on the same queue. The Trainium skill, DMA: Bandwidth & Descriptors, section Queues, rings and completion order, says that descriptors are consumed in ring order on each DMA engine, and here the trace agrees. In the changed kernel the lot is issued from 400.0 on and has landed at about 410.4, 4 us before QT: the mechanism is real, and the change keeps clear of it.

## Why the prediction was right, and where its sizes were off

**What was right and what was luck.** The direction and the mechanism are right, and 605.0 lies in the range of 593 to 607. It lies outside of the 594.5 to 602 that had half of the chance, and the gain, 6.7 us, is about half of the 12.7 to 13.8 forecast. It falls into the interval of the clock's rival, 602 to 605, and that is luck: the clock did not fall in the tail of the profiled execution. What was mis-sized is the work in the merged part.

**What bounds the kernel, and the direction.** Right. By the price list the stage was 25 us longer than its work, and filling it is what won: old_order shows that nothing else in the change does, and cross_last that merged pairs alone do not. The first marks held: TensorE is busy 70.7 of 73.1 us from 331.86 to 405, the clock is 1.00 from 332 to 418.5, no stretch is under a third busy, and the waits from L1 to L2 sum to 1.6 us (0.16, 0.76, 0.16 and 0.50) where about 4 were forecast for TT and L2 and 5.6 stood before. GT, marked at 431, stands at 434.64.

**The merged part: 0.6 + 1.5 forecast, 5.7 measured.** 7Y 3 stands 82.9 us behind the stage's start; 74.7 of work and 2.5 at TT leave 5.7. This is the largest error, and the step that failed is the 74.7, the work, and not the waits. TensorE is busy 79.2 of the 82.9 us and idle 3.6, which is less than the 0.6 + 1.5 + 2.5 = 4.6 put down for waits; the busy time is 4.5 us more than the list has. (A part of that is the end of a matmul that shows as busy when nothing follows it at once; there are seven such waits.) The rows and runs name these sources:
- The price list was too low. G 0 stood in it at "about 0.46"; in the trace of before one takes 0.96 (391.69 to 392.65), and I had estimated it instead of reading it. It is one matmul of 512 columns on unsplit float32 operands, which the trace shows as two instructions, and takes 1.03 (387.76 to 388.79 above); a matmul of the split products of the same width takes 0.24 (339.01 to 339.25). G 2 and Y were priced at 0.87 and 1.43 and take 0.97 (394.85 to 395.82) and 1.52 (400.14 to 401.66). Up to L1 there are one G 0, one G 2 and two Y of pair 7, 0.85 us too little; another of the first two and two Y lie between L1 and TT, about 0.8 us.
- ScalarE's table loads were put at nothing, "as each has 1 to 2 us of TensorE's work ahead of its readers". At CS 0 it had less: cs0_early takes 0.9 us back, and in loads_more two further loads there come through in full (2.6 of 2.6 us), at CS 1 as 2.3 of 2.6. ScalarE's share over the stage, 71.1 of 112.7 us, was the wrong thing to read: the order of its list at that place decides.
- Waits at the start: 0.29 at 6QK 0 (0.6 was forecast), 0.63 at 6E 0, with a VectorE that is busy 16.72 of 19.3 us. I had called these first 16 us "the loop's mixture" and charged nothing. a_first shows that it is VectorE's work and not one badly placed step.

Taken together that is 0.85 + 0.9 + 0.9 = 2.7 us. Some 3 are left over, 0.66 of it at 386.25 before 7Y 0, which the view puts down to "issue"; most of the rest is in no wait, so it is in steps that take longer than their price. No run takes them apart.

**TT: 2.5 forecast, 2.5 measured.** The number agrees, and the reason only in part. From L1 to TT it is 9.49 us with 7.0 of priced work. VectorE is busy 14.57 of the 15.7 us before 7Y 3, as forecast from the eight maxima of [rows 5]. But TensorE idles only 1.2 of these 9.49 us: G 0 and G 2 of the next sequence wait 0.16 and 0.76 for banks that VectorE's maxima still read, 7OT 3 waits 0.16, and at TT itself almost nothing is left. The other 1.3 us are steps that took longer than priced, G 0 first.

**The tail: 18.5 forecast, 19.9 measured.** L2 came 3.8 us behind 7Y 3 (4.2), S3 to GT took 2.9 (3.0), but L2 to S3 13.2 instead of 11.3. The step that failed is "At full clock 5.3 us fewer": it took all half-clock work as lying on the chain. before_keep has the full clock there and is 2.5 us shorter from L2 to GT, not 5.3 (14.2 us from L2 to S3). And the two chains were not even. GpSimd's timeline of the kernel after:

```profile
429.26 0.72 POOL L1746 TENSOR_TENSOR xf_w_lo<-xf_w_raw,xf_w_hi 128x256 fp32r<-128x256 f32 x1
...
431.71 0.56 POOL L1733 TENSOR_TENSOR xf_rstd<-xf_var_eps,xf_minus_half 128x1 f32<-128x1 f32 x1 [1.73 <-DVE xf_var_eps L1548]
```

The fourth WL ends at 429.98, 15.3 us behind 7Y 3, as its chain was priced (15.0). But S3 does not stand right behind it; it waits 1.73 us for VectorE, which has the chain L2, exponentials, AV, OUT. The mark for this step was wrong.

**The clock: 1.1 forecast, 1.0 measured, in another place.** Its rival was half right. In the profiled execution after the clock holds through the tail and falls just at GT, in the first regular turn, where TensorE has work for every microsecond: 6.3 us at 0.50 would be 3.1 us, and 1.0 is seen against after_keep. The other 1.2 us of the rest are the fall near the end, which the profiled execution before has too (1.4 us). In a_first and cs0_early the clock fell inside the tail instead; there L2 to GT takes 18.9 us instead of 16.1, and the fall costs 3.4 us in all (a_first). So its price depends on where it comes. The last sentence of the prediction names a first regular turn that gives time back, but with the wrong cause: not `w_lo_done`, the clock.

**The little DMA (601).** It did not come to that, for the reason that the lot was through 4 us earlier. It was issued from 400.0 on and had landed 10 us later, not 12; QT followed its issue by 14 us.

**Slower, and half density.** The interleaved banks did not stop the lists: the individual waits of E, Y, T and OT in the merged part sum to about 2 us, under the 5 that would have spoken for this rival. From 16 us behind the stage's start to 7Y 3 it is 66.9 us for 58.7 of priced work, a density of 88% by the price list, between the turn's 99% and the 80% of the rival. By TensorE's idle time it is 96% from the stage's start to 7Y 3 (79.2 of 82.9): what was off is more the prices than the order.

**The total.** 98.9 + 3.6 (merged part) + 1.4 (tail) - 1.1 (clock within the stage) = 102.8, as measured. Behind GT it is 0.8 us more than in the profiled execution before: 1.0 + 1.2 for two falls of the clock against 1.4 for one. 614.3 - 10.1 + 0.8 = 605.0, which is the profiled run. The median of before lies 2.6 us under its profiled execution and that of after on it, so the medians differ by 6.7.

## What to carry to other kernels

What is added to a helper engine is priced at its place in that engine's order, by who waits for the next thing in the list; the engine's busy share says nothing about it. A list of prices for an order is made from one row for each kind of step, from its start to the start of the next, the rare ones too: here the list was short by about as much as all the waits together. And when a sum misses, idle time and busy time are compared with it separately; a term that agrees (TT's 2.5) can hide two errors. A stretch at half clock costs what of it lies on the chain, which is less than its missing cycles. When the chain is shortened, the fall may move into the dense work behind it, so the rest of the span has to be compared as well as the stage, at several marks and not only at its end.

## What the runs showed of the hardware

- TensorE's clock falls from 2.4 to 1.2 GHz for some us at a time, in different places in executions of one program. A fall cost 1.0 us in the dense work behind GT (after: 6.3 us at 0.50, so 3.1 us of missing cycles), 1.2 near the end (0.79 over 8 us, 1.7 missing), and 3.4 in the dependent tail (a_first: 0.76 over 18.9 us, 4.5 missing).
- Before the falls TensorE had been waiting a part of the time: 10.85 of 16.1 us busy ahead of GT in after, 3.03 of 4.00 (552 to 556) ahead of the late fall, 2.97 of 5.00 (400 to 405) ahead of the first fall in the kernel before. What decides whether and when it falls in a given run, no experiment shows.
- Matmuls without use raised the mean clock of the kernel before (12 runs at 0.994 to 1.000, against 0.983 to 0.992), but paid nothing there: 613.03 against 611.73 us.
- A DMA of 4 KB behind some 7 MB of transfers on the same queue took 16.56 us instead of 1.78.
- Table loads stand back to back at 1.28 us each, without a drain between them.
- A matmul of 512 columns on unsplit float32 operands (G 0) holds TensorE for 0.93 to 1.03 us, one of the split products for 0.23 to 0.24.
